# Context attention with keys stationary: scores and probabilities kept transposed, maxima subtracted by VectorE, exponentials added by GpSimd

## What is computed

```
q = layernorm(x) @ wq.T                      # 256 x 512
k = concat([ctx, layernorm(x) @ wk.T])       # 4096 + 256 keys
v = concat([ctx, layernorm(x) @ wv.T])       # 4096 + 256 values
attn = softmax(q @ k.T / sqrt(512))          # 256 x 4352
x = x + (attn @ v) @ wo.T
```

## Time and profile before

| | |
|---|---|
| median of three runs | 525.05 us (523.3 to 531.25) |
| time of the profiled execution | 523.41 us |
| its span, first to last instruction | 521.4 us |
| TensorE, busy share | 98% |
| VectorE, busy share | 75% |
| ScalarE, busy share | 58% |
| GpSimd, busy share | 6% |

### The profile page before, as it was taken

One profiled execution on the slowest core, in us unless ns is written; L12 is line 12 of the kernel. 1 busy time (PEld: TensorE's weight loads), 2 busy tenths in 40 slices (PEclk: granted clock), 3 DMA queues, 4 the chain that ended last, 5 costly groups with the idle time before them and its releaser, 6 DMA issues.

```text
span 521.4 us, 9657 instructions
## 1 busy us (share of the span) xinstructions
PE 510.9 (98%) x3454; PEld 458.6 (88%) x3454; DVE 389.1 (75%) x616; ACT 304.4 (58%) x470; POOL 29.4 (6%) x48
## 2 busy tenths in 40 slices
PE   8999999999999999989999999999999999999997
PEld 7988888888777998969899999999999999999997
DVE  6777555557889888867787777677776877778675
ACT  5665586655367776664664655546565465645631
POOL 1000000000524113001000000000000000000000
PEclk9999999999999999999999999999999999999999
DMA  8775634545412233333545464655656555464521
GB/s 290 295 232 174 198 123 132 167 162 158 152 35 77 77 97 145 121 123 137 203 142 194 171 224 155 224 182 180 210 163 229 163 200 201 165 233 152 215 72 40
DMA packets 19459, 86.24 MB, mean 165 GB/s; under 512 B 2160, under 2 KB 2416, under 8 KB 19312
## 3 DMA queue, kind: packets, MB, share of 16 engines
q1 hardware_dynamic: 19440, 85.99, 49.0%
HBM read 85.46 MB, written 0.52 MB: 165 GB/s over the span
## 4 chain that ended last, share of the span: by engine, by line
PE 90%; DVE 5%; ACT 2%; issue 1%; DMA 1%; SPq 0%; ACTq 0%; DVEq 0%
PE bank L936 31%; PE bank L429 17%; PE bank L433 16%; PE bank L432 16%; PE bank L437 2%; PE bank L438 1%; PE bank L439 1%; PE bank L573 1%; DVE w_lo L282 1%; PE bank L715 1%; DMA raw<-wq_dram 1%; PE bank L735 1%; PE bank L696 1%; ACT operands L305 1%; DVE xt_lo L330 1%
## 5 line engine op out<-in xcount | busy, mean ns | idle before, releaser
L277 ACT CAST w_hi<-raw 128x768 fp32r<-128x768 f32 (+3 forms) x158 | 159.0, 1041 | 96.6 <-PE bank L936 82.6
L282 DVE TENSOR_TENSOR w_lo<-raw,w_hi 128x1280 fp32r<-128x1280 f32 (+3 forms) x156 | 182.8, 1213 | 13.8 <-ACT w_hi L277 11.7
L429 PE MATMUL bank<-w_hi,operands 128*128 128x512 f32 (+1 forms) x322 | 125.8, 391 | 1.6 <-DVE operands L330 1.0
L433 PE MATMUL bank<-w_hi,operands 128*128 128x512 f32 (+1 forms) x322 | 124.5, 387 | 0.0
L432 PE MATMUL bank<-w_lo,operands 128*128 128x512 f32 (+1 forms) x322 | 123.8, 385 | 0.0
L936 PE MATMUL bank<-xt_hi,w_lo 128*128 128x256 f32 x512 | 105.3, 277 | 0.0
L936 PE MATMUL bank<-xt_hi,w_hi 128*128 128x256 f32 x512 | 105.3, 277 | 0.0
L936 PE MATMUL bank<-xt_lo,w_hi 128*128 128x256 f32 x512 | 105.1, 277 | 0.0
L936 PEld LDWEIGHTS bank<-xt_hi,w_hi 128*128 128x128 f32 x512 | 81.8, 188 | 2.6
L936 PEld LDWEIGHTS bank<-xt_lo,w_hi 128*128 128x128 f32 x512 | 79.8, 188 | 0.0
L936 PEld LDWEIGHTS bank<-xt_hi,w_lo 128*128 128x128 f32 x512 | 79.7, 188 | 0.0
(11 more groups left out here) (182 smaller groups left out, 563.2 us busy)
## 6 DMA issues: line engine op xcount, KB each, us to landing
raw<-w_exp_dram SPq DMA_DIRECT2D x34, 896.0 KB, 4.7
raw<-w_exp_dram SPq DMA_DIRECT2D x34, 640.0 KB, 5.6
raw<-ctx_t_dram SPq DMA_DIRECT2D x16, 512.0 KB, 4.7
raw<-ctx_n_dram SPq DMA_DIRECT2D x16, 512.0 KB, 4.2
raw<-w_mla_dram SPq DMA_DIRECT2D x8, 512.0 KB, 3.5
raw<-w_mla_dram SPq DMA_DIRECT2D x8, 448.0 KB, 3.8
raw<-wq_dram SPq DMA_DIRECT2D x4, 256.0 KB, 5.2
raw<-wk_dram SPq DMA_DIRECT2D x2, 512.0 KB, 7.1
```

The source lines that it names most:

```text
L277: act.copy(w_hi[:, t.slot, at:at + n], raw[:, t.slot, at:at + n]).then_inc(hi_split[k], 1)
L282: eng.tensor_tensor(w_lo[:, t.slot, at:at + n], raw[:, t.slot, at:at + n], w_hi[:, t.slot, at:at + n].bitcast(F32), ALU.subtract) \
L429: ins = pe.matmul(o, a[0], b[0], start=start, stop=False)
L433: return pe.matmul(o, a[1], b[0], start=False, stop=stop)
```

## The change

The score products swap their operands: 128 keys of the context are stationary and the 256 queries move, so a group is 48 matmuls of 256 columns in place of 24 of 512, and keys lie in the rows of the result, which is the layout that the value product needs. All transposes of probabilities go, and with them the turned copies. The value product swaps too: 128 columns of the context stationary, 256 tokens moving, 48 matmuls of 256 columns a group into four banks, whose result is already the layout for `wo`.

A token's maximum now runs over partitions. VectorE keeps an elementwise maximum over all score tiles in `top_pair`; at the end TensorE turns it, VectorE reduces it, TensorE spreads it over all partitions (`transpose_tops`, `share_tops`, inside the value projection). It can no longer be the bias of the exponential, so VectorE subtracts it from every score tile (`lower`, 1024 columns a group, in place, the maximum read from a bank). ScalarE then takes the exponential in place and rounds it. The row sums are made by GpSimd, which adds each group's exponentials into `total_parts` (`add_up`); TensorE turns the total near the end, and the reciprocal is applied where `wo`'s result is added to the residual (`add_attended`).

The core of the diff (the exponentials of group 0 are done in three pieces ahead of this; the new keys like a small group):

```diff
             def score_group(j, s):
...
-                        ins = product(bank[b][:, :], (q_hi[:, c, half(h)], q_lo[:, c, half(h)]),
-                                      x_chunk(t, c), c == 0, c == NC - 1,
-                                      used[1] if h == c == 0 else None)
+                        for k in range(2):
+                            ins = added(bank[b][:, k * T:k * T + T], x_chunk(t, c, (2 * pair + k) * P, P),
+                                        (q_hi[:, c, :], q_lo[:, c, :]), c == k == 0, c == NC - 1,
+                                        used[1] if pair == c == k == 0 else None)
...
+            def times_context(j, s):
+
+                t = Tile(j, T_CN + s)
+                pe.wait_ge(ev_lo, j * 2 + (V_P1 + s - 1))
+                for k in range(4):
+                    if k % 2 == 0:
+                        ready(t, k // 2)
+                    for m in range(NC):
+                        ins = product(bank[out_banks[m]][:, 0:T], context_chunk(t, k, m),
+                                      (pt_hi[:, s % 2, k, :], pt_lo[:, s % 2, k, :]), False, False)
...
+            def times_last():
...
+                for m in range(NC):
+                    if m == NC - 1:
+                        transpose_totals()
...
-                    exps(s, bass.ds(j * 1024 + (s + 2) * 512, 512), 512, bass.ds(j * 2 + (s + 2), 1))
-                    probs_hi(1 - s, j + (F23["pt_odd"] if s == 0 else F01["pt_even"] + 1))
-                    for k in range(2):
-                        split_hi(act, Tile(j, T_CN + s + 1), k, X_SIZES)
...
+            for g in range(2, NG):
+                t = Tile(0, T_CN + g)
+                v = score_rows[:, g * 1024:g * 1024 + 1024]
+                act.wait_ge(lowered, g + 4)
+                exps(v)
+                split_hi(act, t, 0, X_SIZES)
+
+                act.wait_ge(used[1], t.free(1))
+                probs_hi(g + 4, flat(pt_hi[:, g % 2, :, :]), v)
+                split_hi(act, t, 1, X_SIZES)
...
+            def lower(v, n):
+
+                both = [P, n, T]
+                dve.tensor_tensor(v, v, bank[1][:, T:2 * T].unsqueeze(1).broadcast_to(both), ALU.subtract) \
+                   .then_inc(lowered, 1)
...
-                for s in range(2):
-                    probs_lo(1 - s, j * 4 + (V_PT + 4 + 2 * s))
-                    for k in range(2):
-                        split_lo(dve, Tile(j, T_CN + s + 1), k, X_SIZES)
...
+                for s in (2, 3):
+                    t = Tile(j, T_CN + s)
+                    v = score_rows[:, bass.ds(j * 2048 + s * 1024, 1024)].rearrange("p (k t) -> p k t", t=T)
+                    lower(v, 4)
+                    split_lo(dve, t, 0, X_SIZES)
+                    probs_lo(j * 2 + (V_P1 + s - 1), flat(pt_hi[:, s % 2, :, :]), flat(pt_lo[:, s % 2, :, :]),
+                             score_rows[:, bass.ds(j * 2048 + s * 1024, 1024)])
+                    split_lo(dve, t, 1, X_SIZES)
...
+            def add_up(g):
+
+                pool.wait_ge(p_ready, g + 4)
+                pool.wait_ge(summed, g)
+                pool.tensor_tensor(total_parts, total_parts, by_keys(g * 1024, 4), ALU.add).then_inc(summed, 1)
```

More of the change, by code:

```diff
@@ L579, in times_values @@
-            def times_values(ring, t, number, last=False, midway=None):
-                for h in range(2):
-                    pe.wait_ge(ev_lo, number + h)
+            pe.wait_ge(s_copied, 2 * (NG - 2) + 1)
+            for c in range(NC):
+                for k in range(2):
+                    ins = added(bank[0][:, k * T:k * T + T], (k_hi[:, c, half(k)], k_lo[:, c, half(k)]),
+                                (q_hi[:, c, :], q_lo[:, c, :]), c == k == 0, c == NC - 1,
+                                used[1] if c == k == 0 else None)
@@ L1045, in _ @@
                         split_hi(act, Tile(j, T_CT + s + 1), k, X_SIZES)
[L1046 to L1047 removed]
+                    for pair in range(2):
+                        b = 2 * s + pair
                         act.wait_ge(bank_full[b], j + (F01["s_even"] if s == 0 else F23["s_odd"]))
[L1049 removed]
+                        act.copy(score_rows[:, bass.ds(j * 2048 + (s * 1024 + pair * 512), 512)], bank[b][:, :]) \
@@ L1050, in _ @@
                            .then_inc(s_copied, 1)
-            for h in range(2):
-                act.wait_ge(bank_full[h], F01["s_new"])
-                act.copy(scores[:, h, CTX:KEYS], bank[h][:, 0:T]).then_inc(s_copied, 1)
             for k in range(2):
                 split_hi(act, Tile(0, T_CN), k, X_SIZES)
-            def exps(ring, at, n, sum_at):
-                for h in range(2):
-                    act.activation(probs[:, ring, h, 0:n], scores[:, h, at], ACT.Exp, bias=exp_bias[:, h:h + 1],
-                                   scale=XSCALE, accum_out=sums[:, h, sum_at]).then_inc(p_ready, 1)
@@ L1063, in probs_hi, with exps @@
-            def probs_hi(ring, full, n=512):
-                for h in range(2):
-                    out_hi(act, 2 * ring + h, full, pt_hi[:, ring, h, 0:n], n)
-            act.wait_ge(bias_ready, 1)
-            exps(1, slice(CTX, KEYS), T, slice(NG, NG + 1))
-            exps(0, slice(0, 512), 512, slice(0, 1))
+            act.wait_ge(s_max, 2 * NG + 2)
+            act.copy(flat(new_keys), bank[0][:, :]).then_inc(s_copied, 1)
+            def exps(v):
+                act.activation(v, v, ACT.Exp, scale=XSCALE).then_inc(p_ready, 1)
@@ new lines, in _, with total_rows @@
+            for k in range(2):
+                split_lo(dve, Tile(0, T_WO), k, X_SIZES)
+            def total_rows():
+                dve.wait_ge(summed, NG)
+                dve.tensor_tensor(total_parts[:, 0:2, :], total_parts[:, 0:2, :], total_parts[:, 2:4, :], ALU.add) \
+                   .then_inc(totals, 1)
+                dve.wait_ge(totals, 1)
+                dve.tensor_tensor(total_parts[:, 0, :], total_parts[:, 0, :], total_parts[:, 1, :], ALU.add) \
+                   .then_inc(totals, 1)
+                dve.wait_ge(bank_full[0], F0["sums"])
+                then(dve.tensor_reduce(row_sum[:, :], bank[0][:, 0:T].rearrange("p (h k) -> p h k", h=2), AX, ALU.add))
+                then(dve.reciprocal(row_inv[:, :], row_sum[:, :]))
```

325 lines of the change are left out of this document (191 added, 134 removed).

## The result

The changed kernel takes 537.02 us in the median of four runs (535.83 to 537.46), against 524.98 us for the kernel before on the same chip: a ratio of 1.0186, with a 95% interval from 1.0118 to 1.0255. A second series on another occasion gave 1.0223 (1.0054 to 1.0393). It is slower: both intervals lie above 1, and 2% lies inside both. The profiled execution took 535.83 us with a span of 534.0 us; the forecast for an execution like the profiled one of before was 534.2, and 535.0 as the figure on record.

What follows compares the result with a forecast made beforehand. TensorE bound the kernel before; the changed value loop would wait on VectorE, held by GpSimd. Scores to 63.6, then 7.4, 14.7, 40.4 and 19.0 put the second residual addition at 145.0, +10.8 us: 535.0 us, range 529 to 541.

Steps and rivals of the forecast that it cites:

- hold: Value loop: VectorE's tile half or lo part stands until 0.13 us before the end of GpSimd's 2.39 us addition.
- ring: Value loop: lower, exponential, rounding, half 0, lo part, half 1, next lower; nothing runs ahead, 6.73 us a turn without GpSimd.
- TensorE's gain: Scores and values: 113 ns a product, 5.44 us a group; scores end at 63.6; TensorE alone would save some 8 us.
- TensorE waits for none of them: Scores: 16 elementwise maxima on VectorE replace 16 row maxima of the same width and were costed at nothing.
- VectorE and ScalarE in a group: Value loop, 1024 columns: `lower` 1.22 us (between 1.22 and 1.37), exponential 1.05 (between 1.05 and 1.37).
- GpSimd holds VectorE up: Value loop: the addition blocks VectorE's half 0, making a turn 8.08 us against 6.39 before; TensorE idle 2.6 of each.
- The opening: Value loop start: 14.7 us from the first `lower` to that of group 2, with GpSimd's first two additions holding VectorE.
- What comes behind: After the second addition to the residual: the same list on every engine, so no change in time.
- Rival 1: Value loop: GpSimd's additions do not hold VectorE; turn 6.73, 523 to 524 us, not slower; chance 0.08.
- Rival 2: Value loop: TensorE stays the bound if the ring is shorter than 5.44 us; 515 us, 1.6% faster; chance 0.02.
- Rival 3: Value loop: TensorE's clock falls to 1.2 GHz in the gaps, products 10.9 us a group; 541 us; chance 0.05.
- TensorE waits about 2.6 us a group: Value loop, sign to look for in the profile: TensorE waits that long each group for VectorE's lo part.

Runs made afterwards that it cites:

- additions on VectorE: Changed kernel with all GpSimd additions of exponentials moved to VectorE, behind `lower` of the next group: 532.38 us, ratio 1.0035 to the kernel before.
- additions later: Changed kernel with GpSimd's additions of groups 2 to 6 started only after VectorE split the second half of their tile: 531.14 us, ratio 1.0102 to the kernel before.
- waits filled: Changed kernel with 6 more products (18 matmuls) on TensorE behind each value-loop group, results unread: 541.55 us, ratio 1.0251 to the kernel before.

## Why the prediction was right, point by point

**What bounds it.** The statement that TensorE was the bound and that the question was whether the others keep up was right; with neither hold nor ring the second addition stood 5.1 us earlier than before (129.02 against 134.16).

**TensorE's gain.** In the scores 267 products of 256 columns stand between 30 and 60 us, 112 to 113 ns apart. Those of the new keys, which took 120 before, do so too: 24 of them from 64.69 to 67.29 (timeline of TensorE), 2.60 / 23 = 113 ns. The forecast that the scores end at 63.6 was 1.1 early. What failed here is "TensorE waits for none of them", said of the 16 maxima that I cost at nothing: the maxima themselves show no wait, but they begin with a memset that I had not priced, and it stands on VectorE's list ahead of the second group's split. Rows of VectorE before the change, then of VectorE and TensorE after it:

```profile
24.29 2.36 DVE L282 TENSOR_TENSOR w_lo<-raw,w_hi 128x1024 fp32r<-128x1024 f32 x2
...
24.87 0.48 DVE L1368 MEMSET tops<- 128x512 f32 x1
25.27 2.29 DVE L294 TENSOR_TENSOR w_lo<-raw,w_hi 128x1024 fp32r<-128x1024 f32 x2
...
25.39 0.28 PE L453 MATMUL bank<-operands,w_lo 128*128 128x256 f32 x1
26.48 0.39 PE L449 MATMUL bank<-operands,w_hi 128*128 128x256 f32 x1 [0.82 <-DVE w_lo L294]
```

The split starts at 25.27, before the change at 24.29; 0.4 of this is the memset (24.87 to 25.27), and most of the rest a first context tile that was rounded 0.5 later (17.51 against 17.01). TensorE is idle for 0.82 us; from start to start, 25.39 to 26.48 and 0.23 to the next, the stop costs 1.1 us over a pace of 0.113, which is the whole delay. In the second profile of the changed kernel and in the run with additions on VectorE, where that tile was rounded from 17.21 and 16.91 on, waits of 0.54 and 0.40 were left. That the memset makes what is left is worked out from these rows; no run shows it.

**VectorE and ScalarE in a group.** `lower` with a bank as input took 1.21, the value taken at the lower bound; the exponential of 1024 columns 1.06, also as taken. The ring's 6.73 was measured in three runs without hold: 6.69.

**GpSimd holds VectorE up.** 1.35 us of hold a turn, and 8.05 against 8.08. The rule from three short collisions, "as if begun 0.13 us before GpSimd's end", holds for 1024 against 1024 and for 512 against 1024. The Trainium skill's "SBUF — State Buffer", section "SBUF: two separate sides", says of the shared pair of ports that whoever starts first has it for the whole instruction and the other is blocked; the collisions shown here agree, with VectorE held (2.57 instead of 1.22) and with GpSimd held (3.35 instead of 2.39). The addition took 2.38 to 2.40 us; the estimate of 2.25 from the Trainium skill's "GPSIMD Engine Reference", section "Elementwise — side-by-side cycle accounting", would have been 0.14 short.

**The opening.** 14.59 against 14.7. Its two collisions were there: GpSimd's first addition (3.00, of which 0.6 behind a VectorE half), the lo part of group 1 held for 1.83, the second half for 1.1. Rows of GpSimd and VectorE:

```profile
80.45 3.00 POOL L1825 TENSOR_TENSOR xn<-score_rows 128x1024 f32<-128x1024 f32 x1 [73.78 <-ACT score_rows L1120]
83.53 2.15 POOL L1827 TENSOR_TENSOR xn<-xn,score_rows 128x512 f32<-128x512 f32 x1
...
81.49 3.04 DVE L1399 TENSOR_TENSOR operands<-score_rows,operands 128x1024 fp32r<-128x1024 f32 x1 [0.29 <-ACT operands L1124]
84.46 2.30 DVE L294 TENSOR_TENSOR w_lo<-raw,w_hi 128x1024 fp32r<-128x1024 f32 x1
```

**What comes behind.** I had put it at no change; it was 0.63 us longer, so together with the 1.13 of the late mark the forecast for the profiled execution was some 1.6 us short. The two traces run alike to a mark early in the second attention (158.58 before, 170.57 after), and 0.7 us more pass to the next common mark (224.27 and 236.97), with a wait of TensorE for VectorE, 0.34 us at 206.99, that was not there. No run isolates it, and its cause stays open.

**The rivals.** Rival 1, no hold, gave the right turn for its condition: 6.69 where the additions were made small. Rival 2's 5.44 came true once both the hold and the ring were gone. Rival 3 was half right: the clock does fall, to 0.69 over a turn, behind a wait of 3.39 us (before 93.79), and "its granted clock stays full" in what I said would show was wrong. But its price was wrong too: I had counted slow products on top of a turn that stays full, while they use up the wait of the next group. The row says so: in 94.72:102.76 TensorE is busy for all of the 8.04 us, and the next group waits for nothing. The forecast "TensorE waits about 2.6 us a group" fails with it: 3.39, 0, 1.92, 0.61, 2.34, 0.63. Where the low clock meets the last group it does cost, 1.5 us in one of two profiles of the changed kernel. So the forecast of a full clock failed, and in the profiled execution it cost next to nothing because of where the falls came to lie; nothing in the working had foreseen that, and it was luck. The Trainium skill's "TensorE: Matmul & The Clock Gate", section "Part 1: The HAM clock gate", says that an idle array is throttled; the fall behind 3.39 us agrees with it, while the turn behind a wait of 2.33 us in the second profile read 1.00.

**The range.** 529 to 541 held the time, and its own range of 530 to 540 too. The chances, 0.46 within 2% and 0.52 slower, describe a result that lies on that line.

## What to carry to other kernels

Before GpSimd is given work to relieve VectorE, look at which of VectorE's instructions it will meet: beside one that reads a bank the additions cost nothing, beside one that reads two inputs outside the banks VectorE stands until they end. A chain in which an engine waits for its own result by way of another should run one group ahead; at the second addition to the residual that alone was worth 7.7 us here, the placing of the additions alone 5.8, both together 12.8, and 18.9 with the additions shared and the opening put in order. When the clock falls behind a wait, ask first whether the slow products lie in the slack of the next wait.

## What the runs showed of the hardware that was not expected

TensorE's granted clock fell within one loop and came back in it: 0.88 over the turn that ended in a wait of 3.39 us, 0.69 over the next, in which TensorE worked throughout: its products started 0.213 us apart to 99.50 and 0.113 apart behind it, the lower level (1.2 GHz) and the full one (2.4 GHz). Then it read 0.94, 0.85 behind a wait of 1.92, 1.00, and 0.76 behind a wait of 2.34. In the run "additions later" it read 0.77 over the turn behind a wait of 2.06 us, and 1.00 in the turns behind waits of 0.6 to 1.0. With the waits filled, where the longest was 1.5 us, it read 1.00 throughout. Among the value loop's waits of 1.9 us and more the second profile of the changed kernel has the one exception: 1.00 behind 2.33.

The blocking between VectorE and GpSimd was there for the shortest instruction tried as well: an addition of 8 columns waited 0.95 us (1.16 instead of 0.21) for VectorE's instruction to end.
